# Experts by pairs of 128-row tiles: 256 rows moving against weights as the stationary side

## The reference

```python
logits = flat @ Wr                       # flat: 8192 x 256, Wr: 256 x 8
topv, topi = top_k(softmax(logits), 2);  topv = topv / sum(topv)
w = sum(one_hot(topi) * topv)            # weight of each row for each expert
g = einsum('td,edf->etf', flat, Wg)      # Wg, Wu: 8 x 256 x 512
u = einsum('td,edf->etf', flat, Wu)
a = silu(g) * u
o = einsum('etf,efd->etd', a, Wd)        # Wd: 8 x 512 x 256
out = clip(residual + einsum('te,etd->td', w, o), -100, 100)
```

## Time and profile before

| | |
|---|---|
| median of 3 runs | 3332.89 us (3332.68 to 3335.68) |
| profiled execution | 3336.61 us, span of its instructions 3334.8 us |
| mean granted clock of TensorE | 0.945 of full speed |
| TensorE busy over the span | 2874.7 us, 86% |
| VectorE, ScalarE, GpSimd busy | 65%, 50%, 53% |
| first turns of the expert stage | 2458.00 us from the span's start |
| last down projection of it | 3253.69 us |
| expert stage, TensorE busy / clock between 2472.39 and 3246.73 | 100% / 1.00 |

### The profile page before, as it was taken

How to read it: one execution, slowest core, us unless ns; L and a number is a source line. 1 busy time by engine, 2 the same in 40 slices (tenths; PEclk the granted TensorE clock), 3 DMA queues, 4 the chain that set the end, 5 groups by cost and what they waited for, 6 DMA issues and landing times. The chain is left out here.

```text
span 3334.8 us, 54048 instructions
## 1 busy us (share of the span) xinstructions
PE 2874.7 (86%) x17348; PEld 1708.5 (51%) x17349; DVE 2155.8 (65%) x4620; ACT 1671.5 (50%) x3836; POOL 1764.0 (53%) x2330
## 2 busy tenths in 40 slices
PE   3567899889989989988998997988869999999990
PEld 3344545555555555554554554444336666666660
DVE  3566887888888798789889878757522222222226
ACT  1234657657656666766765765765512222222224
POOL 5686755765775775676676576232132222222225
PEclk8777999999999999999999999999979999999995
DMA  1000000000000000000000000001243333333325
GB/s 46 0 10 10 11 9 13 14 25 13 27 20 16 29 19 19 19 22 24 12 27 22 14 25 17 14 26 58 85 125 55 58 59 57 51 59 57 57 46 205
DMA packets 102670, 123.21 MB, mean 37 GB/s; under 512 B 14384, under 2 KB 90160, under 8 KB 102448
## 3 DMA queue, kind: packets, MB, share of 16 engines
q1 hardware_dynamic: 76720, 85.54, 8.5%
q0 software_dynamic: 25728, 34.88, 6.1%
HBM read 58.23 MB, written 61.36 MB: 36 GB/s over the span
## 5 line engine op out<-in xcount | busy, mean ns | idle before, releaser
L897 ACT ACTIVATE wd<-SP_ 128x512 f32<-128x512 f32 (+3 forms) x1536 | 723.5, 488 | 474.1 <-PE SP_ L1576 334.4
L1194 DVE TENSOR_REDUCE NM<-MX 128x1 f32<-128x512 f32 (+3 forms) x1216 | 762.4, 654 | 244.4 <-PE MX L1533 148.3
L1530 PE MATMUL MX<-KST,QST 96*128 96x512 bf16 (+3 forms) x1536 | 454.7, 334 | 102.7 <-DVE NM L1194 91.1
L560 POOL TENSOR_TENSOR wg<-wu 128x1024 f32<-128x1024 f32 x256 | 487.7, 1925 | 103.8 <-DVE wu L1030 103.6
L1573 PE MATMUL SP_<-QST,KST 99*128 99x512 bf16 (+3 forms) x1536 | 501.7, 333 | 33.6 <-ACT wd L897 16.1
L1790 POOL DMA_INDIRECT scratch_h<-Y,XG x136 | 211.4, 1554 | 601.5 <-DVE Y L1853 504.0
L1831 DVE TENSOR_TENSOR AG<-UB,SL 128x512 f32<-128x512 f32 x136 | 94.1, 692 | 469.3 <-PE UB L1870 469.3
L1808 ACT ACTIVATE SL<-GB 128x512 f32<-128x512 f32 x136 | 81.3, 598 | 603.7 <-PE GB L1870 603.7
L1043 DVE TENSOR_TENSOR wg<-wu,SUM 128x1024 f32<-128x1024 f32 x256 | 310.2, 1212 | 101.2 <-PE SUM L1427 101.2
L1530 PEld LDWEIGHTS MX<-KST,QST 96*128 96x128 bf16 x1536 | 135.1, 98 | 431.5 <-DVE NM L1194 301.3
L1590 PE MATMUL OA<-wd,V 128*32 128x512 f32 (+3 forms) x3072 | 331.9, 504 | 0.9 <-ACT wd L897 0.4
(11 more groups left out here) (246 smaller groups left out, 5001.3 us busy)
## 6 DMA issues: line engine op xcount, KB each, us to landing
XG<-scratch_xs SPq DMA_DIRECT2D x136, 130.0 KB, 2.1
wu<-in_L_attn_x SPq DMA_DIRECT2D x64, 128.0 KB, 2.1
scratch_x<-wu SPq DMA_DIRECT2D x64, 128.0 KB, 1.7
scratch_h<-H SPq DMA_DIRECT2D x64, 128.0 KB, 1.7
X<-scratch_x SPq DMA_DIRECT2D x16, 512.0 KB, 3.9
out<-X SPq DMA_DIRECT2D x16, 512.0 KB, 2.9
wg<-in_L_ffn_Wg SPq DMA_DIRECT2D x8, 512.0 KB, 4.3
wu<-in_L_ffn_Wu SPq DMA_DIRECT2D x8, 512.0 KB, 4.7
```

The source lines that it names most:

```text
L560: sg["prod1"].by(pool.tensor_tensor(P1[:, k // 2, (k % 2) * hh * D:(k % 2 + 1) * hh * D].rearrange("p (h e d) -> p h e d", h=hh, e=HD), QK ...
L897: sg["exp"].by(act.activation(PR[:, n % 8, q0:512], SP_[:, n % 2, q0:512], ACT.Exp))
L1194: sg["mx"].by(dve.tensor_reduce(NM[:, u % 2, part, i, h:h + heads], MX[:, index % 2, 0:heads * n].rearrange("p (h n) -> p h n", n=n), AX.X ...
L1530: m = pe.matmul(out[:, k], QST[0:MROW, j % 2, g * G + h + k, i * P:(i + 1) * P], KST[0:MROW, keys % RK, g, 0:n], start=k == 0, stop=not la ...
```

## The change

The unit of work becomes a pair of tiles, 256 rows, of which there are NPAIRS = 64 + 7 = 71 (142 tiles). In the projections for gate and up the weights become the stationary side: for each of four blocks f of 128 columns of weights, and two chunks of the contraction, one matmul with the 256 rows of XT moving. The results stand with the columns of the weights on the partitions and the rows of x along the free dimension, which is how the down projection needs its stationary side. So the turns of the gated rows (TA), their evacuation (AGT) and the two buffers go. The stationary operands are read from fixed buffers, into which the weights of the pair's expert are first copied: gate weights by ACT into WG, up weights by DVE into WU, 128x1024 each, two buffers each.

```diff
-UNROLL = 8
-NSLOT_TILES = -(-(2 * TT + E - 1) // UNROLL) * UNROLL
+UNROLL = 4
+NPAIRS = TT + E - 1
...
-                    do(dve.tensor_scalar(fill[:, 0], fill[:, 0], float(P - 1), None, ALU.add))
+                    do(dve.tensor_scalar(fill[:, 0], fill[:, 0], float(PAIR - 1), None, ALU.add))
...
-                sp.dma_start(XG[:, s], dram["xs"][bass.ds(row, P), :]).then_inc(sg[f"loaded{s}"].sem, 16)
+                sp.dma_start(XG[:, s], dram["xs"][bass.ds(row, PAIR), :].rearrange("(j p) f -> p j f", p=P))\
+                    .then_inc(sg[f"loaded{s}"].sem, 16)
...
+                for s in range(count):
+                    for j in range(2):
+                        pool.wait_ge(sg["y"].sem, 2 * (n0 + s) + j + 1 + CREDIT)
+                        if not (first and s == 0 and j == 0):
+                            pool.wait_ge(sg["added"].sem, (2 * (n0 + s) + j) * 16)
+                            pool.sem_inc(sg["freed"].sem, 1)
...
+            def silu(n):
+                for b in range(2):
+                    act.wait_ge(sg["g"].sem, 2 * n + b + 1)
+                    act.wait_ge(sg["ag"].sem, 2 * n + b - 1 + CREDIT)
+                    act.activation(SL[:, b], GB[:, b], ACT.Silu).then_inc(sg["silu"].sem, 1)
...
+            def gate_weights(s, n):
+                e = expert(n)
+                act.activation(WG[:, s % 2], wg[:, bass.ds(e, 1)].squeeze(1), ACT.Copy).then_inc(sg["wg"].sem, 1)
...
+            def body(n0, i, count, last):
+                for s in range(count):
+                    if not (last and s + 1 >= count):
+                        silu(n0 + s + 1)
+                    if not (last and s + 2 >= count):
                         x_evac(s, n0 + s + 2)
+                        gate_weights(s, n0 + s + 2)
...
+            def up_weights(s, n):
+                e = expert(n)
+                dve.tensor_copy(WU[:, s % 2], wu[:, bass.ds(e, 1)].squeeze(1)).then_inc(sg["wu"].sem, 1)
...
+                    for j in range(2):
+                        dve.tensor_scalar(Y[:, s % 2, j], DN[:, j], share[:, slot, j:j + 1], None, ALU.mult).then_inc(sg["y"].sem, 1)
+                    if not (last and s + 1 >= count):
+                        gate(n + 1)
+                    if not (last and s + 2 >= count):
+                        up_weights(s, n + 2)
...
+            def project(s, n, w, out, ready, done):
+                pe.wait_ge(sg[ready].sem, n + 1)
+                for b in range(2):
+                    pe.wait_ge(sg["ag"].sem, 2 * n + b - 1 + CREDIT)
+                    for k in range(2):
+                        f = 2 * b + k
+                        for c in range(FC):
+                            m = pe.matmul(out[:, b, k * PAIR:(k + 1) * PAIR], w[:, s % 2, c, f * P:(f + 1) * P],
+                                          XT[:, s % 2, c], start=c == 0, stop=c == FC - 1)
+                    m.then_inc(sg[done].sem, 1)
...
+            def body(n0, i, count, last):
+                for s in range(count):
                     n = n0 + s
+                    more = not (last and s + 1 >= count)
+                    e = expert(n)
                     if more:
                         pe.wait_ge(sg["xT"].sem, n + 2)
+                        project(s + 1, n + 1, WG, GB, "wg", "g")
+                    combine(n, e)
+                    if more:
+                        project(s + 1, n + 1, WU, UB, "wu", "u")
+                    if not (last and s + 2 >= count):
                         turn_x(s + 2, i)
```

More of the change, by code:

```diff
@@ L1771, in _ @@
                 load(s, s)
[L1773 to L1775 removed]
+            def body(n0, i, count, last):
+                for s in range(count - AHEAD if last else count):
+                    sp.wait_ge(sg["freed"].sem, 2 * (n0 + s + AHEAD - U + 1) + SPARE)
                     load((s + AHEAD) % U, n0 + s + AHEAD)
@@ L1783, in _, with body @@
         def _(pool):
[L1784 to L1797, removed]
+            def body(n0, count, first):
+                for s in range(count):
[4 more added lines that the diff above has]
+                            pool.sem_inc(sg["freed"].sem, 1)
+                        pool.indirect_dma_start(
+                            out=dram["h2"], out_offset=bass.IndirectOffsetOnAxis(ap=XG[:, s % U, j, ROW - 1:ROW].bitcast(U32), axis=0),
+                            in_=Y[:, s % 2, j], in_offset=None, compute_op=ALU.add).then_inc(sg["added"].sem, 16)
+            pool.sem_inc(sg["freed"].sem, SPARE)
+            body(0, U, True)
+            with pool.Fori(1, ROUNDS) as i:
+                body(i * U, U, False)
+            body(ROUNDS * U, N - ROUNDS * U, False)
+            pool.wait_ge(sg["added"].sem, 2 * N * 16)
         @block.scalar
@@ L1833, in _, with expert @@
+            def expert(n):
+                at = texpi[0:1, n:n + 1] if isinstance(n, int) else texpi[0:1, bass.ds(n, 1)]
+                return dve.value_load(at, min_val=0, max_val=E - 1)
+            def up_weights(s, n):
+                e = expert(n)
+                dve.tensor_copy(WU[:, s % 2], wu[:, bass.ds(e, 1)].squeeze(1)).then_inc(sg["wu"].sem, 1)
             dve.sem_inc(sg["ag"].sem, CREDIT)
             dve.sem_inc(sg["y"].sem, CREDIT)
-            gate(0, 0)
-            def body(n0, i, last):
-                for s in range(U):
+            dve.wait_ge(wsem, 16 * 3 * E)
@@ L1839, in body @@
+            up_weights(0, 0)
+            up_weights(1, 1)
+            gate(0)
+            def body(n0, i, count, last):
+                for s in range(count):
                     n = n0 + s
-                    first_choice = XG[:, s, D:D + 1]
-                    gain, second = XG[:, s, D + 1:D + 2], XG[:, s, D + 2:D + 3]
+                    slot = s % U
                     here = texp[:, n:n + 1] if isinstance(n, int) else texp[:, bass.ds(n, 1)]
-                    dve.wait_ge(sg[f"loaded{s}"].sem, (i + 1) * 16)
@@ L1844, in body @@
[L1844 to L1850, removed]
-                    dve.wait_ge(sg["share"].sem, n + 1)
@@ L1874, in _, with combine @@
+            def combine(n, e):
+                pe.wait_ge(sg["ag"].sem, 2 * n + 2 + CREDIT)
+                pe.wait_ge(sg["y"].sem, 2 * n + CREDIT)
+                for j in range(2):
+                    for f in range(FK):
+                        m = pe.matmul(DN[:, j], AG[:, f, j * P:(j + 1) * P], wd[:, bass.ds(e, 1), f, :].squeeze(1),
+                                      start=f == 0, stop=f == FK - 1)
+                m.then_inc(sg["down"].sem, 1)
             pe.wait_ge(wsem, 16 * 3 * E)
-            pe.sem_inc(sg["tpa"].sem, CREDIT)
+            pe.sem_inc(sg["down"].sem, CREDIT)
@@ L1876, in _, with body @@
             turn_x(0, 0)
+            pe.wait_ge(sg["xT"].sem, 1)
             turn_x(1, 0)
[L1878 to L1885, removed]
+            project(0, 0, WG, GB, "wg", "g")
+            project(0, 0, WU, UB, "wu", "u")
+            def body(n0, i, count, last):
+                for s in range(count):
@@ L1895, in body @@
[L1895 to L1899, removed]
-                        turn_x(s + 2, i)
-                    if more:
-                        project(s + 1, n + 1, e1, wu, UB, "gu")
-                    pe.wait_ge(sg["agT"].sem, n + 1 + CREDIT)
```

133 lines of the change are left out of this document (65 added, 68 removed).

## The result

The changed kernel takes 3511.98 us (median of 4, 3508.19 to 3516.75) against 3333.64 us: a ratio of 1.0535, 95% interval 1.0517 to 1.0553, so 5.3% slower. The prediction was 3521 us. The profiled execution took 3516.75 us, its span 3514.9, which is 180.1 longer than before.

What follows compares the result with a forecast made beforehand. TensorE alone was taken to bound the expert stage. 69 steps of 13.85 us (10.80 work, 2.20 stall, 0.85 clock), with the stage's first and last parts, gave 3521 us; range 3452 to 3590.

Steps and rivals of the forecast that it cites:

- The stall and its place: TensorE idles before each gate projection from the third pair on, waiting for ScalarE's evacuation and weight copy behind the turns.
- Its size: Idle time on TensorE before a gate projection: 2.20 us a pair, with bounds of 2.04 and 3.02.
- The work of a pair: TensorE's work for two tiles in the expert stage: 10.80 us, 0.84 less than before.
- The clock: One stall in two is followed by TensorE at half speed: 0.85 us a pair, bounds none and 3.2.
- The edges: Start and end of the expert stage: first turns 0.8 us later; closing part 11.4 us after TensorE's end, before 8.2.
- The sum: Whole kernel: 69 steps of 13.85 us plus first and last parts, 188.6 us later than before, 3521 us.
- rival 1: TensorE's clock stays at 1.00 through the stalls: step 12.84 to 13.2 us, time 3451 to 3476 us; chance 0.20.
- Rival 3: Not slower: the chain before the gate projection is covered; without any stall, step 10.80 and time 3311 us; chance 0.04.
- rival 4: GpSimd's scatters bind the expert stage, over 6.5 us each: step 13 us and upwards; chance 0.02.

Runs made afterwards that it cites:

- experiment 1: Changed kernel with TensorE's turns of x for pair n+2 ahead of the up projection instead of behind it: 3318.8 us, ratio 0.9946 to the kernel before.
- 2: Changed kernel with ScalarE's register load and copy of the next gate weights ahead of the two silu instructions: 3388.26 us, ratio 1.0158 to the kernel before.
- 5: Kernel before the change, with TensorE's two turns of x moved behind the down projection, directly ahead of the gate projection: 3441.69 us, ratio 1.0318.
- experiment 4: Changed kernel with ScalarE copying the gate weights a second time, into an unused PSUM tile, ahead of the copy into WG: 3735.04 us, ratio 1.1204.
- experiment 3: Changed kernel with only ScalarE's register load of the expert's number moved ahead of the evacuation of TX: 3466.12 us, ratio 1.0391 to the kernel before.

## Why the prediction was right

- **The stall and its place**: right. Experiments 1 and 2 remove it by order alone, 1 fully and 2 by the part of load and copy, and 5 puts a shorter one into the other kernel. The rule that decided was in the order: what stands directly ahead of a projection and what it waits for.
- **Its size**: 2.38 us at full clock against 2.20 forecast. The evacuation (0.60) and the copy (1.06 against 1.03) were right. The register load left 0.21 on average behind the evacuation where I had 0.16, and TensorE's waking took 0.23 where I had 0.12, which is the larger part. Over 68 steps that is 12 us too little.
- **The work of a pair**: 10.80 us, exact (experiment 1, 734 us without a gap). 256 columns with a fresh weight load cost half of 512. The gain that the change was to bring is there: the first experiment is 17 us under the kernel before in the same comparison (3318.8 against 3335.92).
- **The clock**: the step that was mis-sized. I took one stall in two from four cases of the attention part; it was 16 in 69, 0.40 us a step instead of 0.85, 31 us too much. So the mean clock in the stage was 0.97, and not within the 0.85 to 0.95 that I had named as its sign. That the term exists is shown by the rows at 0.50 above and by experiment 4. The page's rule (Trainium skill, "TensorE: Matmul & The Clock Gate", section "Why this matters for your kernels"), by which a gap this short costs nothing, does not hold here: idle stretches of 2.05 to 2.25 us came with half speed 16 times. Read as a rough guide it points the right way, since at 2.8 to 3.3 us the falls became the rule.
- **The edges**: the first turns were 10 us later than forecast. The last scatter of the attention part started between 2440.39 and 2453.69 over the eight profiles, in code that none of the versions touches; the early end of that spread is experiment 3:

```profile
2440.39 0.96 POOL L651 DMA_INDIRECT scratch_xs<-FX,SLOT  x1 [0.30 <-issue]
```

  The changed kernel's profile happened to be the latest of them, so these 7.7 us are not the change's. The other 3 us were there in each profile with pairs (14.5 to 15.7 from that scatter to the turns): 0.8 is the larger first load, as forecast; the rest fits the padding writes of twice the size (the last five take 7.30 us together where they took 4.76), but that was not tried alone.
- **The sum**: 12 us too little for the stall and 31 too much for the clock make the 68 steps 19 us shorter than forecast; the late start gave 10 back and the third scatter at the end 2, the first and last steps took 2 less. The span is so 8.5 shorter than the forecast 3523.4, and the profiled execution stood 4.8 over the median where I had 3.7. Two errors of opposite sign hid each other, and 3521 against 3512 looks better than its terms.
- **The chances**: rival 1 (the clock stays at 1.00) was refuted for this kernel, and it is what the profile of experiment 3 shows with only 0.3 us less in the stall. Rival 3's price, 3311 us for no stall, came out at 3318.8 once the order was mended; rival 4 did not come up, but with 5.1 us on average from the first to the second scatter of a pair in the changed kernel, 10.2 for two, experiment 1 leaves only 0.6 us a pair.

## What to carry to other kernels

A product that goes out through another engine and comes back needs other work of that engine between its two halves; when such work is removed or merged, look at what now stands directly ahead of the reader, and move the producer up before judging the rest of the change. Here two moved lines turned 5.3% slower into 0.5% faster. And a stall costs more than its own length where the clock reacts: count half-speed stretches separately from idle time, since in the profiles here 0.3 us less in the stall took all of them away, 0.3 us more left 9 of 16, and about 1 us more brought one with nearly every stall.

## What the runs showed of the hardware

- TensorE's granted clock fell in or just behind none of 69 idle stretches of 1.7 to 1.8 us, 16 of 69, most of them 2.04 to 2.39 us, 9 of 69, most of them 2.36 to 2.68 us, and 65 of 69 of 2.8 to 3.3 us. Half speed lasted 3.41 us, or 6.83 us with 58 of the 65.
- A copy of 128x1024 float32 from SBUF to SBUF takes 1.057 us on ScalarE and 0.694 us on VectorE, whose 128x512 product out of PSUM takes 0.692.
- A register load behind an activation of 0.60 us is not wholly hidden by it: 0.03 to 0.45 us, 0.21 on average, remain before the next one that uses the register. With the load ahead, the next one starts 0.10 us before the recorded end of the first.
